# First output projection and norm inside the last attention group, weight splits later

## The chip, the cores and the metric

One core of one Trainium2 chip runs the whole program. The metric is the device time of a launch in microseconds (us), the median of several runs.

## The reference

A post-norm decoder layer on 2 sequences of 1024 tokens, width 256, in float32:

```python
x = _layernorm(x + attn(x, WQ, WK, WV, WO))          # causal, 16 heads of 16
x = _layernorm(x + xattn(x, ctx, ctx, mask, Wq, ...))  # 64 context keys per sequence
x = _layernorm(x + ffn(x, gate_w, gate_b, w13, w2, w13_s, w2_s))
```

The feed-forward part routes each token to 4 of 16 experts (sigmoid scores plus a bias, top 4, weights normalised and scaled by 2.5) and adds a shared expert. An expert is `(silu(x W1) * (x W3)) W2` with an inner width of 128.

## The kernel before

Each engine has its own program, in an order written out by hand, and they meet by semaphores. Tokens lie in 16 tiles of 128, eight for each sequence. The stages are these.

Causal attention runs over NG = 8 groups of four heads, four groups for each sequence. In a group, `step_order` lists 24 "B" steps (score blocks, line 1509), after which ScalarE takes the exponential (792), GpSimd cuts the diagonal blocks (680), and every second step TensorE multiplies by the values ("V", `product`, 1533). Between them stand the row maxima of the next group ("A": TensorE 1492 and 1497, VectorE 957), so the last group has none. Each group's row sums go to DRAM and back (`sums` on SyncE, 493 to 512), with VectorE's reciprocal between ("R" at step 14, line 947), and `normalise` on GpSimd (686, 689) scales the group two groups later, and adds each odd group to the even one before it, raising `o_done`. The last group is scaled and added by VectorE (1051, 1055).

Behind the last group stand the key and value projections of cross-attention (1584, 1588) and the tile loop over all 16 tiles. Per tile t: TensorE's output projection (1608, banks 0 and 1), which needs `o_done` of its sequence; VectorE's residual addition and statistics (`norm_stats`, 1025 to 1031); GpSimd's `power` (714); VectorE's `norm_apply` (1036); TensorE's transpose into a bank (`transpose_x`, 1598, three tiles later); ScalarE's copy into x_T (824); and after every fourth tile a query projection (1624) that ScalarE keeps with its bias (831). VectorE also turns keys and values into block form there, in 20 pieces (`keep_kv`, 1010 and 1018), over tiles 5 to 14.

The expert weights are loaded after the last group (SyncE, 553 to 564). Each of 17 experts (the last is the shared one) is split in two parts: `w_high` on ScalarE (817, two instructions) and then `w_low` on GpSimd (721, two instructions). With W_TILE = 4 and W_LAG = 4, ScalarE splits experts 0 to 11 at tiles 4 to 15, GpSimd 0 to 7 at tiles 8 to 15; the others follow in cross-attention.

Cross-attention runs in the order of `x_order`: 32 steps (two for each tile), each kind of work lagging behind the scores "S" by its number of steps in `LAGS`. ScalarE has an exponential (864) and a copy (871) at each step; GpSimd adds the output bias (740) at the first 16 steps, has a `w_low` at odd steps, and `power` of the second norm at "Y"; VectorE's `norm_shift` (1074) needs this power, ScalarE's apply (881) needs that, and TensorE's transpose "X" (1598) needs the apply. Routing, the scatter of tokens (755), the experts' blocks and the last norm follow.

On each engine an instruction that waits holds up all behind it.

## Time and profile before

| | us |
|---|---|
| median of 3 runs | 721.92 |
| lowest, highest | 718.9, 725.09 |
| the profiled run, its time | 721.0 |
| its span in the trace | 719.2 |
| busy in the span: TensorE | 608.2 (85%) |
| VectorE | 480.7 (67%) |
| ScalarE | 361.3 (50%) |
| GpSimd | 323.4 (45%) |

The share of busy time is an average over stages. For the change, what counts is the stretch from the start of the last group, at about 280.6 us, to the middle of cross-attention, at about 400 us. The largest entries of the chain of waits by line are TensorE's matmuls of lines 1533, 1509 and 1492, those of attention.

### The profile page before, as it was taken

Reading aid. Unit: us, or ns where it says so; the run is one execution under the profiler, and the core shown is the slowest. Engines: PE = TensorE matmul, PEld = TensorE weight load, DVE = VectorE, ACT = ScalarE, POOL = GpSimd, SP = SyncE. Lnnn points to the kernel's source line nnn. Section 1 sums busy time; section 2 is a strip of 40 time slices with the busy share of each in tenths; the row PEclk is TensorE's granted clock in tenths of the full one; section 3 lists DMA queues with packets and bytes.
Section 4 is the critical chain, followed back from the end, with each engine's and each line's share of the span. In section 5 each row is a group of like instructions: output and inputs, shape, how many; then the busy total and the mean of one; then the engine's idle time right before and its main releaser. Section 6 shows DMA issues by size and latency. Waiting matters only on the chain.

```text
span 719.2 us, 12945 instructions
## 1 busy us (share of the span) xinstructions
PE 608.2 (85%) x3852; PEld 370.8 (52%) x3852; DVE 480.7 (67%) x1310; ACT 361.3 (50%) x745; POOL 323.4 (45%) x397
## 2 busy tenths in 40 slices
PE   5888899999999998988799897965345888888874
PEld 2534443444434432255377675755344777777741
DVE  0378878889788783089478856555425776778676
ACT  1322376666665767725465443423313565556552
POOL 8414212335233433629656373746164455555430
PEclk9999999999999999999999996969676999999998
DMA  5866866527246100068000020212154765467756
GB/s 164 175 170 137 161 209 90 81 43 92 53 56 97 27 4 19 17 209 305 1 1 1 0 96 32 88 40 92 55 171 126 204 197 169 138 179 239 239 186 224
DMA packets 52114, 82.51 MB, mean 115 GB/s; under 512 B 11937, under 2 KB 29601, under 8 KB 51745
## 3 DMA queue, kind: packets, MB, share of 16 engines
q1 hardware_dynamic: 45184, 62.26, 35.4%
q0 software_dynamic: 6864, 19.44, 7.4%
q8 instruction: 34, 0.56, 0.3%
q14 instruction: 32, 0.25, 0.1%
HBM read 53.38 MB, written 32.48 MB: 119 GB/s over the span
## 4 chain that ended last, share of the span: by engine, by line
PE 55%; DVE 17%; issue 8%; another core or an unknown queue 6%; ACT 5%; DMA 4%; POOL 3%; SPq 1%; DVEq 0%; ACTq 0%; POOLq 0%
PE ps L1533 9%; PE ps L1509 8%; PE ps L1492 7%; PE ps L1803 6%; DVE neg_max L957 6%; PE ps L1826 5%; PE ps L1699 3%; PE ps L1718 3%; PE ps L1497 2%; PE ps L1782 2%; PE ps L1708 1%; POOL stacks L647 1%; PE ps L1735 1%; DMA expert_parts<-expert_outputs 1%
## 5 line engine op out<-in xcount | busy, mean ns | idle before, releaser
L957 DVE TENSOR_REDUCE neg_max<-ps 128x1 f32<-128x512 f32 (+3 forms) x304 | 181.5, 654 | 41.4 <-PE ps L1497 25.2
L792 ACT ACTIVATE temps<-ps 128x1024 f32<-128x1024 f32 (+1 forms) x192 | 147.5, 812 | 78.0 <-PE ps L1509 78.0
L680 POOL TENSOR_SCALAR_AFFINE_SELECT temps<-temps 128x256 f32<-128x256 f32 x128 | 52.1, 410 | 148.2 <-ACT temps L792 147.2
L1492 PE MATMUL ps<-stacks 96*128 96x512 bf16 (+3 forms) x384 | 104.5, 328 | 10.3 <-DVE neg_max L957 4.7
L762 POOL DMA_INDIRECT expert_outputs<-x_T,w_o_xqkv x79 | 76.1, 963 | 75.6 <-ACT x_T L930 45.0
L1509 PE MATMUL ps<-stacks 99*128 99x512 bf16 (+3 forms) x384 | 93.3, 328 | 2.9 <-DMA stacks<-m_rows 1.4
L1533 PE MATMUL ps<-temps,v_group 128*32 128x512 f32 (+3 forms) x768 | 81.8, 497 | 1.6 <-POOL temps L680 1.0
L755 POOL DMA_INDIRECT expert_slots<-x_tok,w_o_xqkv x64 | 62.4, 974 | 35.4 <-DVE w_o_xqkv L1142 17.9
L1803 PE MATMUL ps<-w_split,block_x 128*128 x474 | 71.3, 287 | 0.8 <-DVE block_x L1379 0.8
L1509 PEld LDWEIGHTS ps<-stacks 99*128 99x128 bf16 x384 | 26.9, 97 | 75.0 <-ACT temps L792 49.6
L1826 PE MATMUL ps<-w_split,block_h 128*128 x237 | 50.7, 323 | 17.5 <-DVE block_h L1406 11.5
L1803 PEld LDWEIGHTS ps<-w_split,block_x 128*128 128x128 f32 x474 | 63.1, 192 | 1.5 <-issue 1.3
L1492 PEld LDWEIGHTS ps<-stacks 96*128 96x128 bf16 x384 | 36.8, 97 | 47.9 <-DVE neg_max L957 21.2
L1402 DVE TENSOR_TENSOR o_norm<-ps,o_norm 128x128 f32<-128x128 f32 x79 | 22.9, 290 | 46.9 <-ACT o_norm L917 35.8
L917 ACT ACTIVATE o_norm<-ps 128x128 f32<-128x128 f32 x79 | 21.9, 278 | 56.1 <-PE ps L1803 33.0
L1826 PEld LDWEIGHTS ps<-w_split,block_h 128*128 128x128 f32 x237 | 34.8, 193 | 29.5 <-issue 26.8
L1497 PE MATMUL ps<-caus_a,ident_b 128*128 128x128 bf16 x256 | 49.8, 221 | 0.0
L714 POOL TENSOR_TENSOR ln_rstd<-ln_var_eps,minus_half 128x1 f32<-128x1 f32 x32 | 19.8, 618 | 65.1 <-DVE ln_var_eps L1031 65.1
L864 ACT ACTIVATE o_norm<-o_norm 128x512 f32<-128x512 f32 x32 | 20.2, 630 | 46.2 <-DVE o_norm L1291 43.5
L930 ACT ACTIVATE x_T<-ps,w_o_xqkv 128x256 f32<-128x256 f32 x60 | 28.6, 477 | 20.3 <-PE ps L1826 16.9
L1547 PE MATMUL ps<-x_T,w_qkv 128*128 128x512 f32 x64 | 32.5, 649 | 7.5 <-DMA x_T<-in_xT 7.5
L1379 DVE TENSOR_TENSOR block_x<-ps,block_x 128x256 fp32r<-128x256 f32 x79 | 33.4, 423 | 7.6 <-issue 3.3
(221 smaller groups left out, 1105.9 us busy)
## 6 DMA issues: line engine op xcount, KB each, us to landing
stacks<-qk_parts SPq DMA_DIRECT2D x96, 128.0 KB, 5.9
v_group<-expert_slots SPq DMA_DIRECT2D x79, 138.5 KB
qk_parts<-temps SPq DMA_DIRECT2D x8, 768.0 KB, 4.4
w_raw<-in_w SPq DMA_DIRECT2D x4, 1024.0 KB, 10.7
early_parts<-expert_outputs SPq DMA_DIRECT2D x4, 1024.0 KB
expert_slots<-in_pad SPq DMA_DIRECT2D x16, 138.5 KB
expert_slots<-in_pad SPq DMA_DIRECT2D x1, 2077.5 KB
x_T<-in_xT SPq DMA_DIRECT2D x4, 512.0 KB, 7.6
```

The costliest lines, as they stand in the source:

```text
L680: nc.gpsimd.affine_select(diag, diag, [[0, 2], [1, P]], ALU.is_ge, zero, base=0, channel_multiplier=-1).then_inc(b_cut, 1)
L755: pool.indirect_dma_start(slots, bass.IndirectOffsetOnAxis(ridx[:, t, k:k + 1].bitcast(U32), 0), xe[:, t, :], None).then_inc(scattered[q], 16)
L762: pool.indirect_dma_start(sums_of, bass.IndirectOffsetOnAxis(idxs[:, b:b + 1].bitcast(U32), 0), yb[:, b % YB, :], None).then_inc(landed[b ...
L792: nc.scalar.activation(pt[:, n % 4, :, 0:w], ps[:, 2 + 2 * (n % 2):4 + 2 * (n % 2), 0:w], ACT.Exp, scale=SCALE).then_inc(b_exp, 1)
L957: nc.vector.tensor_reduce(nmx[:, c, h0:h0 + nh, i], ps[:, A_BANKS[n % 3], 0:w * nh].rearrange("p (h k) -> p h k", h=nh), axis=AX.X, op=ALU ...
L1379: nc.vector.tensor_tensor(xsp[b % 3][:, 1].rearrange("p k s -> p (k s)"), ps[:, b % 2, 0:D], xsp[b % 3][:, 0].rearrange("p k s -> p (k s)" ...
L1492: last = nc.tensor.matmul(ps[:, A_BANKS[n % 3], w * s:w * s + w], qs[0:KR, ua, h0 + s, P * i:P * i + P], ks[0:KR, ua, h0 + s, CH * c:CH * ...
L1497: last = nc.tensor.matmul(ps[:, A_BANKS[n % 3], w * (s + 1) - P:w * (s + 1)], identb[:], causA[:], start=False, stop=True)
L1509: last = nc.tensor.matmul(ps[:, bank, 0:w], ks[0:KM, u, 2 * pr + s, P * j:P * j + P], qs[0:KM, u, 2 * pr + s, q0:q0 + w], start=True, stop ...
L1533: last = nc.tensor.matmul(ps[HS * h:HS * h + HS, 6, CH - w:CH], vg[:, u, j, h, :], pt[:, (2 * p + h // 2) % 4, h % 2, 0:w], start=(j == 0) ...
L1803: last = nc.tensor.matmul(ps[:, 2 + b % 2, 0:D], xsp[b % 3][:, xp, k, :], w13s[:, bass.ds(expert[b], 1), wp, at:at + 2 * INTER], start=(k ...
L1826: last = nc.tensor.matmul(ps[:, 6 + b % 2, 0:D], hsp[:, b % 3, hp, :], w2s[:, bass.ds(expert[b], 1), wp, :], start=(n == 0), stop=(n == 2))
```

## The change

Tiles 0 to 7 (the first sequence, whose groups are complete) are taken into the last group: at odd steps n, tile (n-1)/2 gets "LY" (projection and statistics), tile (n-3)/2 "LZ" (apply), tile (n-5)/2 "LX" (transpose into bank 7, copied to x_T by VectorE, not by ScalarE). GpSimd's `power` stands behind the diagonal cuts of the same steps, and the scaling of group 5 at step 8. The reciprocal "R" of group 6 keeps step 14. The tile loop runs over tiles 8 to 15 alone. Before it, TensorE makes the first two query projections and VectorE all 20 `keep_kv` pieces, the reciprocal and the two passes over the last group. W_TILE becomes 12 and W_LAG 1: ScalarE splits experts 0 to 3 in the tile loop and 4 to 16 in cross-attention, GpSimd 0 to 2 and 3 to 16, two experts at each odd step up to 13.

Functions that are only moved are left out of the diff (`power`, `norm_stats`, `norm_apply`, `transpose_x` are unchanged).

```diff
--- before.py
+++ after.py
@@ -123,6 +123,8 @@
             out.append(("V", (n - 3) // 2))
         if n == 2 * C0 + 1:
             out.append(("O", 0))
+        if g == NG - 1 and n % 2:
+            out += [(kind, (n - at) // 2) for kind, at in (("LY", 1), ("LZ", 3), ("LX", 5)) if 0 <= n - at < 2 * TB]
     return out
 
 
@@ -441,7 +443,6 @@
 
             return (1, b // 4 + 1) if b % 4 == 3 else (0, b + 1 - (b + 1) // 4)
 
-        KV_TILES = (5, 15)
         LN3_BASE = 2 * NT
         ADDS = ((0, 4), (4, 2), (6, 2), (8, 4), (12, 2), (14, 2))
         FINAL8 = NB1 + E
@@ -454,7 +455,7 @@
             t, n = ADDS[c]
             return lineb[c - 1][:] if c in (1, 2) else accb[:, :, t:t + n, :]
         STATS_END = [3 * LN3_BASE + sum(2 * n + 1 for _, n in ADDS[:c + 1]) for c in range(len(ADDS))]
-        W_TILE, W_LAG = 4, 4
+        W_TILE, W_LAG = 12, 1
         W_ACT, W_POOL = NT - W_TILE, NT - W_TILE - W_LAG
         SHARED = E
 
@@ -688,7 +689,12 @@
                     pool.wait_ge(o_scaled, g + 1)
                     nc.gpsimd.tensor_tensor(on[:, g, :], on[:, g, :], on[:, g - 1, :], ALU.add).then_inc(o_done, 1)
 
-            for g in range(NG):
+            def power(n):
+                pool.wait_ge(ln_chain, 3 * n + 3)
+                nc.gpsimd.tensor_tensor(rstd[:, n % 4:n % 4 + 1], ve[:, n % 4:n % 4 + 1], half[:],
+                                        ALU.pow).then_inc(ln_pow, 1)
+
+            for g in range(NG - 1):
                 for n in DIAG[:2 * C0]:
                     cut(g, n)
                 if 1 <= g < NG - 2:
@@ -701,6 +707,13 @@
                     normalise(g - 2)
                 for n in DIAG[2 * C0:]:
                     cut(g, n)
+            for n in range(NB):
+                if n in DIAG:
+                    cut(NG - 1, n)
+                if n == 2 * C0:
+                    normalise(NG - 3)
+                if n % 2 and 0 <= n - 3 < 2 * TB:
+                    power((n - 3) // 2)
             normalise(NG - 2)
             pool.wait_ge(vg_ready, NG)
             pool.wait_ge(pv_done, NV * NG)
@@ -709,11 +722,6 @@
                 pool.wait_ge(filled, 9 + d)
                 nc.gpsimd.memset(vbd[S2 * d:S2 * d + S2, :, :, VW * d + DH:VW * d + VW], 1.0).then_inc(filled, 1)
 
...
             def w_low(e):
 
                 pool.wait_ge(w_hi, 2 * e + 2)
@@ -727,7 +735,7 @@
                 nc.gpsimd.tensor_tensor(xs_l[:, :, CH * c:CH * c + CH], xT[:, :, CH * c:CH * c + CH],
                                         xs_h[:, :, CH * c:CH * c + CH], ALU.subtract).then_inc(xs_lo, 1)
 
-            for t in range(NT):
+            for t in range(TB, NT):
                 power(t)
                 if t >= W_TILE + W_LAG:
                     w_low(t - W_TILE - W_LAG)
@@ -738,8 +746,9 @@
                 if kind == "S" and n < NT:
                     pool.wait_ge(xT_kept, n + 1)
                     nc.gpsimd.tensor_tensor(x[:, n, :], x[:, n, :], bo, ALU.add).then_inc(bo_added, 1)
-                if kind == "S" and n % 2 and W_POOL + n // 2 <= E:
-                    w_low(W_POOL + n // 2)
+                if kind == "S" and n % 2:
+                    for e in range(W_POOL + n - 1, min(W_POOL + n + 1, E + 1)):
+                        w_low(e)
                 if kind == "Y":
                     power(NT + n)
                 if kind == "M":
@@ -816,7 +825,16 @@
                 for raw, high in zip(raw_of(e), part_of(e, 0)):
                     nc.scalar.activation(high, raw, ACT.Copy).then_inc(w_hi, 1)
 
-            for t in range(NT + 1):
+            def keep_query(c):
+
+                for o in range(2):
+                    act.wait_ge(xq_ready, 2 * c + o + 1)
+                    nc.scalar.activation(q2[:, o, CH * c:CH * c + CH], ps[:, 6 + o, :],
+                                         ACT.Identity, bias=bq[:, o:o + 1]).then_inc(xq_kept, 1)
+
+            keep_query(0)
+            keep_query(1)
+            for t in range(TB, NT + 1):
                 if W_TILE <= t < NT:
                     w_high(t - W_TILE)
                 if t < NT:
@@ -824,12 +842,9 @@
                     nc.scalar.activation(xT[:, :, P * t:P * t + P],
                                          ps[:, 2 + t % 2, 0:D].rearrange("p (c s) -> p c s", c=KC),
                                          ACT.Copy).then_inc(xT_kept, 1)
-                if t and t % 4 == 0:
-                    for o in range(2):
-                        n = (t // 4 - 1) * 2 + o
-                        act.wait_ge(xq_ready, n + 1)
-                        nc.scalar.activation(q2[:, o, CH * (t // 4 - 1):CH * (t // 4)], ps[:, 6 + o, :],
-                                             ACT.Identity, bias=bq[:, o:o + 1]).then_inc(xq_kept, 1)
+                if t > TB and t % 4 == 0:
+                    keep_query(t // 4 - 1)
+
             def shared(c):
                 act.wait_ge(g_ready, c + 1)
                 wait(act, h_done, c - 1)
@@ -862,8 +877,9 @@
                     if n >= 2:
                         act.wait_ge(xpT_ready, n - 1)
                     nc.scalar.activation(px[:, n % 2, :], sx[:, n % 2, :], ACT.Exp, scale=SCALE).then_inc(xp_exp, 1)
-                    if n % 2 and W_ACT + n // 2 <= E:
-                        w_high(W_ACT + n // 2)
+                    if n % 2:
+                        for e in range(W_ACT + n - 1, min(W_ACT + n + 1, E + 1)):
+                            w_high(e)
                 if kind == "T":
                     act.wait_ge(xpT_ready, n + 1)
                     if n >= 2:
@@ -942,6 +958,25 @@
         @block.vector
         def _(dve):
             dve.wait_ge(filled, 7)
+
...
             def recip(g, slot):
                 dve.wait_ge(l_moved, 48 * g + 32)
                 nc.vector.reciprocal(lrec[:, slot, :], lsum[:, slot, :]).then_inc(l_recip, 1)
@@ -959,6 +994,17 @@
                                                 axis=AX.X, op=ALU.max, negate=True).then_inc(a_max, 1)
                     if kind == "R":
                         recip(g - 1, (g - 1) % 3)
+                    if kind == "LY":
+                        if n == 0:
+                            dve.wait_ge(ld_late, 16 * 16)
+                        dve.wait_ge(y_ready, n + 1)
+                        norm_stats(n, ps[:, n % 2, 0:D], n, n % 4)
+                    if kind == "LZ":
+                        norm_apply(n, n, n % 4)
+                    if kind == "LX":
+                        dve.wait_ge(xT_ready, n + 1)
+                        nc.vector.tensor_copy(xT[:, :, P * n:P * n + P],
+                                              ps[:, 7, 0:D].rearrange("p (c s) -> p c s", c=KC)).then_inc(xT_kept, 1)
                     if kind == "M":
 
                         base = (g + 1) * 4
@@ -1018,46 +1064,21 @@
                     nc.vector.tensor_tensor(vbd[rows, b, :, VW * d:VW * d + DH], src, bias,
                                             ALU.add).then_inc(kv_kept, 1)
 
...
-            for t in range(NT + 1):
-                if KV_TILES[0] <= t < KV_TILES[1]:
-                    span = KV_TILES[1] - KV_TILES[0]
-                    at = t - KV_TILES[0]
-                    for piece in range(20 * at // span, 20 * (at + 1) // span):
-                        keep_kv(piece)
-                if t == 1:
-                    dve.wait_ge(l_moved, 48 * (NG - 1) + 32)
-                    nc.vector.reciprocal(lrec[:, (NG - 1) % 3, :], lsum[:, (NG - 1) % 3, :]).then_inc(l_recip, 1)
-                if t == 6:
-
-                    dve.wait_ge(l_spread[(NG - 1) % 2], 64 * (NG // 2))
-                    nc.vector.tensor_tensor(on[:, NG - 1, :], on[:, NG - 1, :], rl[:, (NG - 1) % 2, :],
-                                            ALU.mult).then_inc(o_scaled, 1)
-                if t == 7:
-                    dve.wait_ge(o_scaled, NG)
-                    nc.vector.tensor_tensor(on[:, NG - 1, :], on[:, NG - 1, :], on[:, NG - 2, :],
-                                            ALU.add).then_inc(o_done, 1)
+            for piece in range(4):
+                keep_kv(piece)
+            recip(NG - 1, (NG - 1) % 3)
+            for piece in range(4, 20):
+                keep_kv(piece)
+            dve.wait_ge(l_spread[(NG - 1) % 2], 64 * (NG // 2))
+            nc.vector.tensor_tensor(on[:, NG - 1, :], on[:, NG - 1, :], rl[:, (NG - 1) % 2, :],
+                                    ALU.mult).then_inc(o_scaled, 1)
+            dve.wait_ge(o_scaled, NG)
+            nc.vector.tensor_tensor(on[:, NG - 1, :], on[:, NG - 1, :], on[:, NG - 2, :], ALU.add).then_inc(o_done, 1)
+            for t in range(TB, NT + 1):
                 if t < NT:
                     dve.wait_ge(y_ready, t + 1)
                     norm_stats(t, ps[:, t % 2, 0:D], t, t % 4)
-                if t >= 1:
+                if t > TB:
                     norm_apply(t - 1, t - 1, (t - 1) % 4)
 
             steps = [0]
@@ -1474,6 +1495,32 @@
 
         @block.tensor
         def _(pe):
+            def transpose_x(t, bank):
+                for k in range(KC):
+                    last = nc.tensor.transpose(ps[:, bank, P * k:P * k + P], x[:, t, P * k:P * k + P], identf[:])
+                last.then_inc(xT_ready, 1)
+
+            def out_project(t):
+
+                pe.wait_ge(o_done, (t // TB + 1) * GB // 2)
+                if t >= 2:
+                    pe.wait_ge(ln_in, t - 1)
+                for q in range(GB // 2):
+                    pair = on[:, t // TB * GB + 2 * q + 1, P * (t % TB):P * (t % TB) + P]
+                    last = nc.tensor.matmul(ps[:, t % 2, 0:D], pair, wo1[:, q, :], start=(q == 0),
+                                            stop=(q == GB // 2 - 1))
+                last.then_inc(y_ready, 1)
+
+            def query_project(c):
+
+                for o in range(2):
+                    if c:
+                        pe.wait_ge(xq_kept, 2 * c + o - 1)
+                    for k in range(KC):
+                        last = nc.tensor.matmul(ps[:, 6 + o, :], wxq[:, k, P * o:P * o + P],
+                                                xT[:, k, CH * c:CH * c + CH], start=(k == 0), stop=(k == KC - 1))
+                    last.then_inc(xq_ready, 1)
+
             def group(g, order):
 
                 u = g % 3
@@ -1509,6 +1556,16 @@
                             last = nc.tensor.matmul(ps[:, bank, 0:w], ks[0:KM, u, 2 * pr + s, P * j:P * j + P],
                                                     qs[0:KM, u, 2 * pr + s, q0:q0 + w], start=True, stop=True)
                         last.then_inc(b_ready, 1)
+                    if kind == "LY":
+                        if n == 0:
+                            pe.wait_ge(ld_late, 16 * 16)
+                            pe.wait_ge(a_max, NA * NG)
+                            pe.wait_ge(m_row, NG)
+                        out_project(n)
+                    if kind == "LX":
+                        pe.wait_ge(ln_done, n + 1)
+                        wait(pe, xT_kept, n)
+                        transpose_x(n, 7)
                     if kind in ("V", "Vp"):
                         product(g * NV + (0 if kind == "V" else -NV), g if kind == "V" else g - 1,
                                 u if kind == "V" else (g - 1) % 3, n)
@@ -1593,37 +1650,21 @@
             pe.wait_ge(o_kept, 2 * NG)
             pe.wait_ge(m_row, NG)
 
...
+            pe.wait_ge(xT_kept, TB)
+            query_project(0)
+            query_project(1)
+            for t in range(TB, NT + 4):
                 if t < NT:
-                    if t >= 2:
-                        pe.wait_ge(ln_in, t - 1)
-                    pe.wait_ge(o_done, (t // TB + 1) * GB // 2)
-                    for q in range(GB // 2):
-                        pair = on[:, t // TB * GB + 2 * q + 1, P * (t % TB):P * (t % TB) + P]
-                        last = nc.tensor.matmul(ps[:, t % 2, 0:D], pair, wo1[:, q, :], start=(q == 0),
-                                                stop=(q == GB // 2 - 1))
-                    last.then_inc(y_ready, 1)
+                    out_project(t)
                 s = t - 3
-                if 0 <= s < NT:
+                if TB <= s < NT:
                     pe.wait_ge(ln_done, s + 1)
-                    if s >= 2:
-                        pe.wait_ge(xT_kept, s - 1)
+                    pe.wait_ge(xT_kept, max(s - 1, TB))
                     transpose_x(s, 2 + s % 2)
                 s -= 1
-                if s >= 0 and s % 4 == 3:
+                if s >= TB and s % 4 == 3:
                     pe.wait_ge(xT_kept, s + 1)
-                    for o in range(2):
-                        if s >= 4:
-                            pe.wait_ge(xq_kept, s // 4 * 2 + o - 1)
-                        for k in range(KC):
-                            last = nc.tensor.matmul(ps[:, 6 + o, :], wxq[:, k, P * o:P * o + P],
-                                                    xT[:, k, P * (s - 3):P * (s + 1)], start=(k == 0), stop=(k == KC - 1))
-                        last.then_inc(xq_ready, 1)
+                    query_project(s // 4)
 
             def project(c, part):
 
```

## Rows read from the trace of the kernel before

**Rows 1.** Busy time by engine, stretch by stretch: a full group, then the last group.
```profile
222.90:251.75 28.85, 28.02 (x220) 11.73 (x217) 23.34 (x44) 19.21 (x27) 11.49 (x18) 1.00 0.49 67
...
280.60:303.80 23.20, 20.35 (x153) 5.37 (x153) 1.07 (x2) 18.86 (x26) 12.06 (x19) 1.00 0.05 14
```

**Rows 2.** Timeline, TensorE in the tile loop: start us, us, engine, line, operation.
```profile
323.56 0.38 PE L1598 MATMUL ps<-ident_f,x_tok 128*128 128x128 f32 x2
...
323.78 1.03 PE L1608 MATMUL ps<-w_o_xqkv,o_norm 128*128 128x256 f32 x4
...
324.64 0.38 PE L1598 MATMUL ps<-ident_f,x_tok 128*128 128x128 f32 x2
```

**Rows 3.** Timeline inside the last group: GpSimd's normalisation of group 5, ScalarE's exponentials.
```profile
288.45 2.35 POOL L686 TENSOR_TENSOR o_norm<-o_norm,temps 128x1024 f32<-128x1024 f32 x1
...
290.57 3.85 ACT L792 ACTIVATE temps<-ps 128x1024 f32<-128x1024 f32 x4
```

**Rows 4.** Row sums of the last group: timeline, and the landing time of L511.
```profile
303.91 0.60 ACT L807 ACTIVATE o_norm<-ps 128x512 f32<-128x512 f32 x1 [1.19 <-PE ps L1533]
...
310.68 1.71 SPq L511 DMA_DIRECT2D temps<-row_sums  x4
...
DMA to landing us min/median/max: 2.1/2.5/3.5
```

**Rows 5.** Timeline of the tile loop: key/value products, VectorE's tile, keep_kv, scaling, one query block.
```profile
304.77 1.89 PE L1588 MATMUL ps<-w_o_xqkv,ctx_T 128*128 128x256 f32 x8
...
310.60 0.42 DVE L1025 TENSOR_TENSOR x_tok<-ps,x_tok 128x256 f32<-128x256 f32 x1
...
312.12 0.42 DVE L1025 TENSOR_TENSOR x_tok<-ps,x_tok 128x256 f32<-128x256 f32 x1
...
315.17 0.72 DVE L1010 TENSOR_SCALAR v_group<-ps,b_k,head_mask 128x128 f32<-128x128 f32 x2
...
317.96 1.22 DVE L1051 TENSOR_TENSOR o_norm<-o_norm,temps 128x1024 f32<-128x1024 f32 x1
...
338.91 3.60 PE L1624 MATMUL ps<-x_T,w_o_xqkv 128*128 128x512 f32 x8
```

**Rows 6.** Timeline of the end of the tile loop, and its two stretches by engine.
```profile
342.55 0.69 ACT L831 ACTIVATE o_norm<-ps,b_q 128x512 f32<-128x512 f32 x1 [1.03 <-PE ps L1624]
...
343.13 0.92 ACT L817 ACTIVATE w_split<-w_raw 128x512 fp32r<-128x512 f32 x2
...
343.91 2.00 POOL L721 TENSOR_TENSOR w_split<-w_raw,w_split 128x512 fp32r<-128x512 f32 x2
...
343.98 1.35 DVE L1036 TENSOR_SCALAR x_tok<-x_tok,ln_mean_var,ln_rstd 128x256 f32<-128x256 f32 x1 [1.13 <-POOL ln_rstd L714]
...
346.57 5.28 PE L1624 MATMUL ps<-x_T,w_o_xqkv 128*128 128x512 f32 x8 [0.75 <-ACT x_T L824]
...
352.83 1.10 PE L1699 MATMUL ps<-v_group,o_norm 128*128 128x512 f32 x2 [0.97 <-ACT o_norm L831]
...
346.50:352.00 5.50, 5.28 (x8) 2.08 (x8) 0.00 (x0) 0.81 (x3) 0.08 (x1) 0.70 0.00 0
```

**Rows 7.** Timeline of the start of cross-attention, up to its second tile's transpose.
```profile
352.24 1.41 POOL L740 TENSOR_TENSOR x_tok<-x_tok,w_qkv 128x256 f32<-128x256 f32 x2
...
357.49 0.92 ACT L817 ACTIVATE w_split<-w_raw 128x512 fp32r<-128x512 f32 x2
...
371.02 0.55 POOL L714 TENSOR_TENSOR ln_rstd<-ln_var_eps,minus_half 128x1 f32<-128x1 f32 x1 [5.94 <-DVE ln_var_eps L1031]
...
372.30 0.63 ACT L864 ACTIVATE o_norm<-o_norm 128x512 f32<-128x512 f32 x1 [1.46 <-DVE o_norm L1291]
...
373.57 0.60 ACT L881 ACTIVATE x_tok<-x_tok,ln_minus_mean,ln_rstd 128x256 f32<-128x256 f32 x1
...
375.30 0.38 PE L1598 MATMUL ps<-ident_f,x_tok 128*128 128x128 f32 x2
...
381.37 0.38 PE L1598 MATMUL ps<-ident_f,x_tok 128*128 128x128 f32 x2
```

39 lines of the change are left out of this document (15 added, 24 removed).

## The prediction

> **What bounds the kernel now.** I read the forty slices of the page first, for where TensorE is full; then the chain of waits, for which lines carry the time around the change; then stretches by engine; then the timeline of the same stretches. [rows 1] shows, behind each stretch's length, the busy time of TensorE's matmuls, its weight loads, VectorE, ScalarE and GpSimd, then the granted clock: a full attention group has TensorE busy for 28.02 of 28.85 us. The last group builds no maxima for a next one: 20.35 of 23.20 us, VectorE 1.07, ScalarE 18.86 [rows 1]. So it has 2.85 us of idle TensorE and an almost empty VectorE, the room that the change fills. The group ends at 303.8 [rows 1], cross-attention's first score is at 352.83 [rows 6]: 49.0 us of tile loop, in which VectorE's chain per tile sets the pace, 1.52 us from one addition to the next (310.60 to 312.12) [rows 5]. In cross-attention TensorE is the bound: 6.07 us a tile, from transpose to transpose (375.30 to 381.37) [rows 7].
>
> **Step 1, the last group grows.** TensorE gets eight output projections and eight transposes. Behind one another they take 323.56 to 323.78 for the transpose and 323.78 to 324.64 for the projection, so 1.08 us a tile [rows 2], 8.6 us for eight. Walked through in its new order, the first projection falls into a wait for ScalarE and costs nothing (0.9 back). From step 4 to 19 TensorE is behind instead, since two full exponentials take 1.9 us (3.85 for four) [rows 3] and what TensorE does meanwhile is over 3 us; there all is paid. Two of the x_T copies, which VectorE makes in order behind the next tile's statistics, come 0.3 us late (0.6 more), and of the other 1.95 us idle about half, 0.9, is filled while TensorE is behind: 8.6 - 0.9 + 0.6 - 0.9 = **+7.4 us**. Bounds: all idle time filled, 8.6 - 2.85 = +5.8, and 1 less if products also overlap better; +10 if normalise stalls it. GpSimd does that at step 8: 2.35 us [rows 3] and an addition over as many elements, 4.7 us together, ahead of power(3). I place power(3)'s result within 0.5 us of where the transpose of tile 3 is due, so the stall is small, but behind it in TensorE's queue stand the next scores, and for these ScalarE waits. ScalarE itself loses nothing: it has no added instruction there.
>
> The row of one apply shows another meeting: it took 1.35 us beside GpSimd's subtraction of 343.91 [rows 6]. [...]
>
> **Step 2, what the first eight tiles covered.** Group 7's row sums go over DRAM and back: ScalarE's copy at 303.91, the spread issued from 310.68 for 1.71 us, landing 2.5 us after its last issue (about 312.0): 314.5 [rows 4]. That is 10.7 us after the group's end, and about 10.0 when the reciprocal no longer stands behind tiles' statistics. Before, the tiles hid it all. Now TensorE has the key/value products (to 304.77 + 1.89 = 306.7, 2.8 us after the end, its last 0.1 overlapping what follows) and two query blocks, 3.5 us each (3.60 for a block with its tail) [rows 5]: busy to +9.7. VectorE has twenty keep_kv pieces of about 0.36 us (0.72 for two) [rows 5], done by +10.2: these are hidden by the chain. Then the two passes over the whole group, 1.22 us each [rows 5], and o_done at +12.7. TensorE stands still for 3 us.
>
> **Step 3, tiles 8 to 15.** First addition at +13.9, the others every 1.52 us [rows 5]: tile 15's at +24.2, its statistics by +25.3 if nothing stood in the way. But the wait moves to the splits. The loop's ScalarE order is w_high(0), copy 12, keep_query(2), w_high(1). The third query block cannot start before the copy of tile 11, +23.2, and ends at +26.7; keep_query takes 0.69, w_high(1) 0.92 [rows 6]: +28.4. With W_LAG at 1, GpSimd has w_low(1) in front of power(15), where before it was four experts behind and never waited. 2.00 us [rows 6] later power(15), 0.6: +31.0. The apply takes 0.4 to 1.35 [rows 6] beside w_low(2), the transpose and copy 1.2, the last query block 5.28 at the low clock [rows 6], and one more us to the first score (351.85 to 352.83): **+39.0 us** where it was 49.0, so **-10.0**. Bounds: with the last block at the full clock and the apply undisturbed +36.5 (-12.5), and one us better still if VectorE's tiles run below 1.52; +40.5 (-8.5) if the clock is low from the 3 us standstill on.
>
> [...]
>
> **Step 4, cross-attention takes the splits.** ScalarE's splits there go from 5 experts to 13, GpSimd's from 9 to 14, two at every odd step up to 13. GpSimd per tile: two additions of bo 1.41, two splits 4.0 (2.00 each [rows 6]), power 0.55 [rows 7]: 5.8 to 6.0 us against 6.07 [rows 7]. It only just fits, and the start does not: in front of power(16) stand eight bo additions and eight splits. 352.24 to 353.6 the first two additions, w_low(3) to 355.6, then w_low(4) waits for w_high(4), which ends at about 358.5 since ScalarE starts splits at 357.49 [rows 7]; w_low(4) is done at 360.5, three more rounds of two additions and two splits, 5.3 us each, end at 376.4, and power(16) is done at 376.9 instead of 371.57 [rows 7]. ScalarE's apply needs it; it ran at 373.57 and could have run at 374.3 without TensorE's transpose at 375.30 [rows 7] moving, given that a projection is in front of it. With about 1.0 us by which ScalarE's double splits delay the first steps, the transpose comes at 377.7 to 378.3. Behind that wait in TensorE's queue is the next tile's score; behind VectorE's wait for power(16) are the maxima of step 9. One later round adds 0.4. **+3.0 us** (bounds: +1, if ScalarE's and GpSimd's idle time takes it, to +6, the whole 5.3 of GpSimd's lateness and a little).
>
> In the later stretches nothing is added, and since TensorE is full there a shift goes through to the end. Of the eight experts' splits that leave the tile loop nothing is counted on ScalarE, where copies waited for transposes; GpSimd's part of their gain is in step 3.
>
> **The sum.** +7.4 - 10.0 + 3.0 = +0.4 us on the profiled span of 719.2 us, whose run took 721.0; on the median 721.92, 722.3. I say **722 us**. About 1%, 7.2 us, is what a measurement of this kernel can tell from no change.
>
> **Rivals.**
> (a) No measurable change, as above: 0.60. For it: three terms of like size and opposite sign. It holds where the terms stay within their bounds, 716.5 to 727.
> (b) Faster, 713: the idle time of the last group is all filled (+5.3), the loop ends at full clock with the splits out of the way (-13.5), cross-attention pays 1. Sum -7.2 to -9. For it: VectorE is 95% idle in the last group [rows 1]. Against: keep_query(2) stands before w_high(1). 0.17.
> (c) Slower, 729: ScalarE. The second split stands between the exponential of an odd step and the copy that TensorE's next product needs. ScalarE waited 1.46 us before the exponential of step 8 [rows 7]; the second split takes 0.92 of it [rows 6]. If at a step less than 0.92 is left, TensorE stops there, and once a tile: 7 x 0.92 = 6.4 more, 722.3 + 6.4 = 728.7. It decides where ScalarE's idle time per tile falls under 0.92; the 1.46 speaks against. 0.23, with other losses of the same sign.
> The range reaches from (b) to (c): 714 to 729. Likeliest alone: 716.5 to 727. Faster by over 1% 0.17, within 1% 0.60, slower by over 1% 0.23.
>
> **What would show it.** Step 1: the last group's length, 30 to 31 us; its ScalarE idle before exponentials with TensorE as releaser. Under 28.5 or over 33 it is wrong. Step 2: an idle stretch of TensorE of about 3 us after the second query block, ended by VectorE's addition (line 1055 before). Step 3: power(15) starting as w_low(1) ends, and 39 us from group's end to first score. Step 4: power of the first cross tile starting at once behind a split, some 24 us after GpSimd's first bo addition, VectorE waiting for it, and a period of 6.1 us after. What breaks the forecast: a group that swallows the tiles in under 5 us, or cross-attention whose period goes to 7.

## The result and the profile after

| | kernel before, us | changed kernel, us | ratio, 95% interval |
|---|---|---|---|
| median of 7 runs each | 722.9 | 729.61 | 1.0097 [1.0068, 1.0126] |
| lowest, highest | 718.9, 725.09 | 725.9, 733.33 | |
| span of the profiled execution | 719.2 | 727.5 | |

The change costs 6.7 us where 0 was forecast: just outside the range. The same two kernels on another chip gave 1.0118 [1.0032, 1.0203].

The spans by stage, read from the timelines. "First score" is the first of cross-attention; X0, X1 and "last X" are TensorE's transposes of its first, second and last tile, counted from the first score.

| kernel | last group | group's end to first score | X0 | X1 | last X |
|---|---|---|---|---|---|
| before | 23.2 | 49.1 | +22.5 | +28.5 | +141.5 |
| changed | 30.7 | 40.2 | +27.3 | +35.6 | +148.9 |
| difference | +7.5 | -8.9 | +4.8 | +7.1 | +7.4 |

7.5 - 8.9 + 7.4 = 6.0 of the profiled spans' 8.3; most of the rest (2.5) arises in the expert stage, whose length from its first product with split weights to the end was 196.6 and 191.6 us in two profiles of the changed kernel. A second profile of the kernel before, on another chip (before_again), has 23.2, 50.4, +22.5, +28.5 and +139.7: the stretch to the first score and the last X vary by 1 to 2 us in one and the same kernel, the other columns hardly. First the group and what follows, by engine (length, then busy time of TensorE, its weight loads, VectorE, ScalarE, GpSimd, and the granted clock), as in [rows 1]:

```profile
280.30:311.00 30.70, 29.35 (x201) 13.40 (x201) 16.85 (x50) 19.02 (x26) 16.32 (x27) 1.00 0.05 11
343.00:351.10 8.10, 6.69 (x10) 2.63 (x10) 0.00 (x0) 1.76 (x3) 1.39 (x3) 0.64 0.08 33
```

The group holds 9.0 us more TensorE work than in [rows 1], and 1.5 us of its idle time went into that. The timeline of the loop's end, answering to [rows 5, 6]:

```profile
322.17 1.23 DVE L1076 TENSOR_TENSOR o_norm<-o_norm 128x1024 f32<-128x1024 f32 x1
323.45 4.06 PE L1510 MATMUL ps<-w_o_xqkv,o_norm 128*128 128x256 f32 x16 [2.75 <-DVE o_norm L1076]
324.62 0.42 DVE L966 TENSOR_TENSOR x_tok<-ps,x_tok 128x256 f32<-128x256 f32 x1 [1.22 <-PE ps L1510]
...
339.09 1.96 POOL L729 TENSOR_TENSOR w_split<-w_raw,w_split 128x512 fp32r<-128x512 f32 x2 [2.67 <-ACT w_split L826]
341.00 0.56 POOL L694 TENSOR_TENSOR ln_rstd<-ln_var_eps,minus_half 128x1 f32<-128x1 f32 x1
...
341.59 1.35 DVE L977 TENSOR_SCALAR x_tok<-x_tok,ln_mean_var,ln_rstd 128x256 f32<-128x256 f32 x1 [4.72 <-POOL ln_rstd L694]
...
344.15 6.00 PE L1520 MATMUL ps<-x_T,w_o_xqkv 128*128 128x512 f32 x8 [0.47 <-ACT x_T L842]
```

GpSimd's w_low(1) waits 2.67 us for ScalarE, power(15) stands right behind it, and VectorE's last apply waits 4.72 us for that power. The last query projection then takes 6.00 us, at a stretch's clock of 0.64. The start of cross-attention, answering to [rows 7], and the same three instructions at its second tile:

```profile
356.80 1.95 POOL L729 TENSOR_TENSOR w_split<-w_raw,w_split 128x512 fp32r<-128x512 f32 x2 [2.93 <-ACT w_split L826]
...
370.12 3.88 POOL L729 TENSOR_TENSOR w_split<-w_raw,w_split 128x512 fp32r<-128x512 f32 x4
373.94 0.56 POOL L694 TENSOR_TENSOR ln_rstd<-ln_var_eps,minus_half 128x1 f32<-128x1 f32 x1
374.46 1.41 POOL L748 TENSOR_TENSOR x_tok<-x_tok,w_qkv 128x256 f32<-128x256 f32 x2
375.81 1.96 POOL L729 TENSOR_TENSOR w_split<-w_raw,w_split 128x512 fp32r<-128x512 f32 x2
...
374.54 3.25 DVE L1095 SCALAR_TENSOR_TENSOR ln_minus_mean<-ln_mean_var,ln_rstd 128x1 f32<-128x1 f32 x1 [3.18 <-POOL ln_rstd L694]
...
377.82 0.60 ACT L897 ACTIVATE x_tok<-x_tok,ln_minus_mean,ln_rstd 128x256 f32<-128x256 f32 x1 [5.04 <-DVE ln_minus_mean L1095]
...
378.48 0.69 PE L1500 MATMUL ps<-ident_f,x_tok 128*128 128x128 f32 x2 [3.92 <-ACT x_tok L897]
378.96 1.92 PE L1740 MATMUL ps<-v_group,o_norm 128*128 128x512 f32 x2
...
382.60 0.55 POOL L694 TENSOR_TENSOR ln_rstd<-ln_var_eps,minus_half 128x1 f32<-128x1 f32 x1
383.12 1.23 POOL L748 TENSOR_TENSOR x_tok<-x_tok,w_qkv 128x256 f32<-128x256 f32 x2
...
383.18 0.59 DVE L1095 SCALAR_TENSOR_TENSOR ln_minus_mean<-ln_mean_var,ln_rstd 128x1 f32<-128x1 f32 x1 [0.43 <-POOL ln_rstd L694]
```

Read it downwards: the power of the first tile is done 22.8 + 0.6 us behind the first score instead of 18.2 + 0.6. VectorE then makes one column of numbers, 128x1 (`norm_shift`, "the shift" below), and it takes 3.25 us, while GpSimd's two additions (374.46) and the two halves of a split (375.81) run beside it, one behind the other; it ends at 377.79, as GpSimd runs out of work at 377.77. In the kernel before it took 0.15:

```profile
372.18 0.15 DVE L1074 SCALAR_TENSOR_TENSOR ln_minus_mean<-ln_mean_var,ln_rstd 128x1 f32<-128x1 f32 x1
```

The first tile is an exception, though. At the second tile GpSimd's two additions also stand one behind the other, and the shift ends with the first of them, after 0.59 us. At the first tile ScalarE's apply waits for the shift, TensorE stands still ahead of the transpose for 3.92 us, and what follows runs slower, at a granted clock of 0.51 from 376.1 to 383.0: the scores of line 1740 take 1.92 us where they took 1.10 before [rows 6]. X1 comes 8.3 us behind X0, not 6.07 [rows 7]. The third and the fourth tile come 6.1 us apart again, as before the change.

### The profile page after: what moved, and what is told of

Same layout as the page of the kernel before. It is cut to its first block, busy times and chain, and to the rows that moved or that the text cites. A ratio compares the mean times of both kernels' runs of the same rounds, so it can differ in the third digit from the quotient of the medians.

```text
span 727.5 us, 12948 instructions
## 1 busy us (share of the span) xinstructions
PE 609.2 (84%) x3852; PEld 373.9 (51%) x3852; DVE 486.0 (67%) x1318; ACT 359.4 (49%) x737; POOL 323.0 (44%) x397
## 4 chain that ended last, share of the span: by engine, by line
PE 56%; DVE 15%; issue 7%; POOL 6%; another core or an unknown queue 6%; DMA 5%; ACT 4%; SPq 1%; DVEq 0%; ACTq 0%; POOLq 0%
PE ps L1590 9%; PE ps L1556 8%; PE ps L1539 7%; PE ps L1844 6%; DVE neg_max L992 5%; PE ps L1867 5%; PE ps L1740 2%; PE ps L1759 2%; PE ps L1510 2%; POOL w_split L729 2%; PE ps L1823 2%; PE ps L1544 2%; POOL stacks L648 1%; PE ps L1520 1%
## 5 line engine op out<-in xcount | busy, mean ns | idle before, releaser
L1423 DVE TENSOR_TENSOR o_norm<-ps,o_norm 128x128 f32<-128x128 f32 x79 | 22.8, 289 | 47.9 <-issue 23.5
```

## The experiments

The runs went to several chips. On one kind (kind A here: this result, the first four experiments, and before_again, after_again, warm4 and before_shift) the kernel before takes 718 to 723 us, on the other (kind B: all others) 673. Every ratio is to the kernel before on the same chip. Both kinds agree up to the eighth tile of cross-attention; the difference behind it is told in the last section. The changed kernel itself was timed on kind A alone, tiles_only and shadow on kind B alone.

**The splits of cross-attention.** Three edits, and the weights' part alone.

```diff
 single_both: one expert at an odd step on both engines
-                    for e in range(W_POOL + n - 1, min(W_POOL + n + 1, E + 1)):
+                    for e in range(W_POOL + n // 2, min(W_POOL + n // 2 + 1, E + 1)):
                         w_low(e)
 (and the same for w_high); act_double: that for w_low alone
 ...
 shift_first: the changed kernel, with
                     power(NT + n)
+                    pool.wait_ge(ln_shift, n + 1)
 ...
 weights_only: the kernel before, with W_TILE, W_LAG = 12, 1 and two experts at odd steps
```

> The changed kernel, but in cross-attention each engine splits one expert at an odd step (ScalarE up to step 25, GpSimd up to step 27) instead of two. The group and the tile loop stay. Theory (the loss sits in GpSimd's doubled splits in front of the first power of cross-attention, and in what VectorE's norm_shift then waits for): from the first cross score to the transpose of cross tile 1 it takes about 28.5 us as before the change, not 35.6, and the time falls to 722 to 725 us, less if five splits among the scatters cost nothing, more by up to 10 if all do. Rival (the loss is in the group and the tile loop or is spread): 728 to 730, the stretch 33 us or more.

> The changed kernel with ScalarE's splits doubled as they are, GpSimd's one at an odd step. Theory (GpSimd): like single_both within 1 us, stretch from first score to second transpose about 29 to 30 us, 723 to 726 us. Rival (ScalarE's second split between exponential and copy holds TensorE): that stretch stays above 33 us and the time at 728 to 730.

> The changed kernel, and GpSimd waits behind each cross power until VectorE's norm_shift of that tile is done, so that no GpSimd work on SBUF runs beside it. Theory: norm_shift took 3.25 us at cross tile 0 because additions and a split held it up; it falls to about 0.2 us, the first cross transpose comes about 3 us sooner, 726 to 727 us. Rival (norm_shift's 3.25 us is only how a wait is recorded, or GpSimd's own delay gives it back): no change, 729 to 730.

> The kernel before with the later splits alone (W_TILE 12, W_LAG 1, two experts at an odd step); all 16 tiles stay in the tile loop. Theory: the tile loop loses GpSimd's splits from eight tiles and shortens by 4 to 7 us (from group's end to first score 42 to 45 us, not 49), cross-attention pays about 7: 722 to 726 us. Rival (the splits cost nothing in cross-attention by themselves, only together with the tiles): 715 to 718.

| kernel | group | to first score | X0 | X1 | last X | ratio |
|---|---|---|---|---|---|---|
| single_both | 30.7 | 41.0 | +22.5 | +28.5 | +145.2 | 1.004 [1.0012, 1.0068] |
| act_double | 30.7 | 42.7 | +23.3 | +29.3 | +142.8 | 1.0026 [0.9988, 1.0063] |
| shift_first | 30.7 | 40.8 | +24.3 | +30.5 | +145.9 | 1.0014 [0.998, 1.0048] |
| weights_only | 23.2 | 50.8 | +27.4 | +35.7 | +148.9 | 1.0144 [1.0096, 1.0192] |

The steps between these kernels take 6.9 of the 7.1 us of X1 apart. Single splits on both: nothing lost (22.5, 28.5). ScalarE's doubles: 0.8 (23.3). GpSimd's doubles, with VectorE's shift kept clear of them: 1.0 more (24.3). The shift beside GpSimd's work: 3.0 more (27.3). The step from X0 to X1: 6.2 in shift_first, 8.3 in the changed kernel, 2.1 more. In shift_first the same instruction takes 0.16 us, with GpSimd's additions held until it is done:

```profile
375.97 0.16 DVE L1096 SCALAR_TENSOR_TENSOR ln_minus_mean<-ln_mean_var,ln_rstd 128x1 f32<-128x1 f32 x1 [3.18 <-POOL ln_rstd L694]
...
376.21 1.40 POOL L748 TENSOR_TENSOR x_tok<-x_tok,w_qkv 128x256 f32<-128x256 f32 x2 [0.27 <-DVE ln_minus_mean L1096]
```

So GpSimd's work beside the shift is the cause of its 3.25 us. Why it lasted over four instructions is open: all six profiles in which the first power stands behind the doubled subtractions and GpSimd does not wait for the shift show 3.25 or 3.26 us at the first tile, and nowhere else. In the 99 other cases in all these profiles in which an arithmetic operation of GpSimd was running as a shift began, the shift ended within 0.1 us of the end of that operation, whatever stood behind it.

Two limits of this table. The first three kernels run the changed kernel's code up to the first score, and still need 40.8 to 42.7 us where it needed 40.2: behind the standstill ahead of tile 8 the first sixteen products took 4.06 us in the changed kernel and in shift_first, 5.41 in the other two:

```profile
327.47 5.41 PE L1510 MATMUL ps<-w_o_xqkv,o_norm 128*128 128x256 f32 x16 [3.53 <-DVE o_norm L1076]
```

This line is act_double's; the granted clock was 0.53 from 327.5 to 330.0, and 1.00 over the 4.06 us of the changed kernel. And behind the second tile all three lose again, last X +142.8 to +145.9 for +141.5 and +139.7 in the kernel before, which these runs don't take apart.

weights_only missed my expectation on its loop, which I had thought would get shorter. It has the changed kernel's wait in the tile loop too: ScalarE reaches w_high(1) late, and VectorE's last apply stands behind it.

```profile
344.42 1.34 DVE L1038 TENSOR_SCALAR x_tok<-x_tok,ln_mean_var,ln_rstd 128x256 f32<-128x256 f32 x1 [4.05 <-POOL ln_rstd L714]
```

So the weights' part alone costs 1.4%, more than the whole change, and the tiles' part gives back about 0.5% of it, though the two intervals overlap.

**TensorE's clock behind the standstill.** warm and warm4 put 14 and 4 products of 512 columns, results not used, ahead of TensorE's wait for X0 (the edit of warm4; in warm 14 stands for 4):

```diff
                 if kind == "X":
+                    for _ in range(4 if n == 0 else 0):
+                        nc.tensor.matmul(ps[:, 7, :], q2[:, 0, 0:P], kbd[:, 0, 0].rearrange("p h k -> p (h k)"),
+                                         start=True, stop=True)
                     pe.wait_ge(ln_done, NT + n + 1)
```

> The changed kernel with 14 more matmuls of 512 columns on TensorE (results not used) ahead of its wait for the first cross-attention tile's normalised rows, in the standstill of 3.92 us there. Theory (of the delay of the first cross tiles 2.1 us is TensorE's clock, which is at the lower level behind the standstill, so that the second tile comes 8.3 us behind the first instead of 6.1): with TensorE busy until shortly before the transpose, the first transpose stays at 27 to 28 us behind the first score, the second follows after 6.1 to 6.8 us instead of 8.3, and the later tiles stand about 2 us sooner; the time falls by 0 to 2 us, to 727.5 to 729.6. Rival (the 8.3 us come from the queues behind VectorE and ScalarE, whatever the clock): the distance stays 8 us or more.

> The changed kernel with 4 instead of 14 more products of 512 columns (results not used) on TensorE ahead of its wait for the first cross-attention tile: the 14 ran 12.18 us and so held the engine themselves, 4 take 3.5 us, less than the standstill of 3.92 us. Theory (2.1 us of the first tiles' delay is TensorE's clock behind the standstill): the first transpose stays at 27 to 28 us behind the first score, the second follows after 6.1 to 6.8 us and not 8.3, and the time is 0 to 2 us below that of the changed kernel. Rival (the 8.3 us come from the work queued on VectorE and ScalarE, whatever the clock): the distance stays 8 us or more.

warm says nothing on the clock: I had mis-sized the filler, which took 12.18 us and itself put X0 at +35.3 (ratio 1.0172 [1.0123, 1.0221]). warm4 (kind A) settles it:

```profile
377.29 3.60 PE L1781 MATMUL ps<-v_group,o_norm 128*128 128x512 f32 x8
381.37 0.44 PE L1500 MATMUL ps<-ident_f,x_tok 128*128 128x128 f32 x2 [0.48 <-ACT x_tok L897]
381.64 1.02 PE L1740 MATMUL ps<-v_group,o_norm 128*128 128x512 f32 x2
```

X0 at +27.4 as before the filler, X1 at +33.6: 6.2 us and not 8.3, and line 1740 back at 1.02 us; the granted clock was 1.00 from 377.0 to 387.6. Work that computes nothing gave 2.1 us back. (Its profile reached the first score after 42.1 us, with 6.38 us for the sixteen products named above, so the gain is read from X0 to X1 and not from the sum.) Beside it on the same chip ran the changed kernel:

> The changed kernel, word for word, beside the others on the same chip. Theory (the change costs what it costs in the attention, whatever the expert stage takes): the last group 30.7 us, the loop 40.2, the first transposes 27.3 and 35.6 us behind the first score, and a ratio to the kernel before of about 1.010 (the 6.7 us of the first chip). Rival (the quicker chip hides or shows another part of it): a ratio of 1.005 or less, or of 1.015 or more.

It showed 30.7, 40.2, +27.3 and +35.7 and a ratio of 1.0118 [1.0032, 1.0203], warm4 1.007 [1.0027, 1.0113]: the right direction and size, but the two times can't be told apart.

**The wait in the tile loop.** late_power: all powers first, then the three subtractions.

```diff
             for t in range(TB, NT):
                 power(t)
-                if t >= W_TILE + W_LAG:
-                    w_low(t - W_TILE - W_LAG)
+            for e in range(NT - W_TILE - W_LAG):
+                w_low(e)
```

> One edit to the changed kernel: behind the tile loop's copies GpSimd computes all eight powers of the second batch's tiles first and only then the three subtractions of the weight splits, so power(15) no longer stands behind w_low(1), which waits for ScalarE's w_high(1). Theory (the loop gave 8.9 and not more because VectorE's last apply waited 4.72 us for that power): the wait of 4.72 us is gone, the last query projection starts some 4 to 5 us sooner, the stretch from the end of the last group to the first score falls from 40.2 to 35 to 37 us, and the time falls from 729.6 to about 725. Rival (ScalarE's 0.92 us splits and copies set the end of the loop anyway, or the projection then runs longer at the lower clock): the stretch stays above 39 us and the time at 728 to 730. Cross-attention starts with the same double splits, so its tiles should stay where they were, the first transpose of a tile 27 us behind the first score and the second 35 us behind it.

```profile
338.41 1.35 DVE L977 TENSOR_SCALAR x_tok<-x_tok,ln_mean_var,ln_rstd 128x256 f32<-128x256 f32 x1 [0.44 <-POOL ln_rstd L694]
...
341.66 0.94 ACT L826 ACTIVATE w_split<-w_raw 128x512 fp32r<-128x512 f32 x2
342.49 0.38 ACT L842 ACTIVATE x_T<-ps 128x256 f32<-128x256 f32 x1
...
342.92 5.29 PE L1520 MATMUL ps<-x_T,w_o_xqkv 128*128 128x512 f32 x8 [1.69 <-ACT x_T L842]
```

The 4.72 us are gone (0.44), yet the stretch is 38.2, 2.0 shorter and not 3 to 5: the last query projection starts 1.2 us sooner and takes 5.29 us for 6.00. The wait moved to ScalarE, whose last copy stands behind three splits of 0.9 us: the rival was half right. Ratio, kind B: 1.0062 [1.0015, 1.0108]; whether that is a gain isn't shown, since the changed kernel was not timed there.

**The tiles' part with the splits spread out.** W_TILE, W_LAG = 8, 4 and one expert at an odd step; run twice on kind B, the second time with a profile of the kernel before beside it.

> The tiles' part of the change with as little of the weights' part as the shorter loop leaves: ScalarE makes 8 high parts in the loop's tiles 8 to 15, GpSimd 4 low parts with a lag of 4 tiles, and cross-attention makes one of each at an odd step, as before the change. Theory (the tiles' part gains and the weights' part costs): the last group stays 30.7 us, the loop falls to 36 to 39 us (no power behind a subtraction that waits), the first transposes of cross-attention stand 22.5 and 28.5 us behind the first score as before, and the time is 716 to 720, below the kernel before. Rival (the eight tiles in the group cost as much as they save): the time is 722 or more even with the splits spread out.

> The tiles' part of the change with the splits spread out, for a second time. Theory (it gains about 4 us by the first score and loses them in cross-attention's later tiles, where VectorE and GpSimd carry routing, scatters and the splits that the shorter loop pushed behind it): the first score comes 3 to 5 us before that of the kernel before on this chip, the transposes of the first four tiles stand alike, and the last stands 3 to 6 us later behind the first score; the ratio is 1.000 to 1.006. Rival (the loss lies behind the last tile or in the expert stage): the last transpose stands within 1.5 us of that of the kernel before, and the stretches behind it are longer. Second rival (the loss on the other chip was the scatter of the runs): the ratio is 0.993 to 0.997.

| kernel | group | to first score | X0 | X1 | last X | ratio |
|---|---|---|---|---|---|---|
| before_third | 23.2 | 49.2 | +22.5 | +28.5 | +130.4 | |
| tiles_only | 30.7 | 37.6 | +22.5 | +28.5 | +137.9 | 1.0053 [1.0022, 1.0083] |
| tiles_again | 30.7 | 39.7 | +22.5 | +28.5 | +138.0 | 1.0056 [1.0019, 1.0093] |

2.0 to 4.1 us sooner at the first score, alike for four tiles, then 7.5 us lost. My forecast of a time below the kernel before fell: the splits that the shorter loop pushes on end at step 25 on GpSimd (step 17 before), where its queue holds routing's scatters and the powers. Ninth to tenth tile of tiles_again, 11.4 us for 7.5; the shift takes 2.30 us beside GpSimd's 128x1024 subtraction:

```profile
438.73 1.95 POOL L729 TENSOR_TENSOR s_split<-s_raw,s_split 128x512 fp32r<-128x512 f32 x2
440.64 0.57 POOL L694 TENSOR_TENSOR ln_rstd<-ln_var_eps,minus_half 128x1 f32<-128x1 f32 x1
441.19 2.33 POOL L735 TENSOR_TENSOR x_low<-x_T,x_high 128x1024 fp32r<-128x1024 f32 x1
...
441.24 2.30 DVE L1095 SCALAR_TENSOR_TENSOR ln_minus_mean<-ln_mean_var,ln_rstd 128x1 f32<-128x1 f32 x1 [2.12 <-POOL ln_rstd L694]
...
444.23 0.69 PE L1500 MATMUL ps<-ident_f,x_tok 128*128 128x128 f32 x2 [2.02 <-ACT x_tok L897]
```

Another 2.5 us (1.7 in tiles_only) stand between the fourth and the fifth tile, where TensorE was busy throughout and the granted clock fell all the same, to 0.50 from 398 to 402. By stretch, the kernel before (before_third) and then tiles_again:

```profile
394.10:410.40 16.30, 15.80 (x104) 11.94 (x103) 13.40 (x48) 7.01 (x16) 5.34 (x5) 1.00 0.01 2
```

```profile
391.50:407.80 16.30, 16.30 (x90) 12.48 (x88) 11.45 (x39) 8.74 (x20) 6.93 (x7) 0.79 0.00 1
```

Why is open. Over the same 16.3 us the granted clock was 0.90 in tiles_only and after_again and 0.79 in before_shift_again, below; the first profile of the changed kernel, the same program as after_again, lost nothing there (7.8 us from the fourth to the fifth tile, as in the kernel before). So these 1.7 to 2.5 us can't be put down to the tiles' part; the other 5 to 6 us come later.

**A layout of the splits.** shadow: powers first; four subtractions behind them, beside the last query projection; six high parts at ScalarE's tiles 11 to 16; in cross-attention two experts at steps 1, 3 and 5 (ScalarE at 5: one), then one at an odd step to 17 and 19.

```diff
+        W_TILES = {11: (0,), 12: (1,), 13: (2,), 14: (3,), 15: (4,), 16: (5,)}
 ...
+            for e in range(4):
+                w_low(e)
```

> The changed kernel with the splits laid where the engines stand: powers first in the loop, four low parts behind them beside the last query projection, six high parts in ScalarE's tiles 11 to 16, and in cross-attention two at steps 1, 3 and 5 and one at an odd step after these. Theory (the double splits cost where they stand ahead of the first tile's power and additions, at steps 7 and later, not at steps 1 to 5, in which no tile of cross-attention is normalised yet): the stretch from the group to the first score is 33 to 36 us, the first transposes stand at 22.5 to 23.5 and 28.5 to 29.5 us behind the first score as in the kernel before, and the time is 713 to 718. Rival (the doubles at steps 1 to 5 hold ScalarE's exponentials and so the first scores): the first transposes stand at 25 us or more and the time is 720 or more.

> The splits laid beside the last query projection and at cross-attention's steps 1, 3 and 5, for a second time. It reached the first score 35.2 us behind the last group and its last transpose stood 132.6 us behind the first score. Theory (its splits are out of the way before the routing begins): the last transpose stands 2 us or more sooner behind the first score than in the tiles' part alone, the ratio is again 0.990 to 0.998. Rival (the first result was the scatter of the runs): 1.000 or more.

> The changed tiles' order with the splits laid beside the last query projection and at cross-attention's steps 1, 3 and 5. On a chip on which the kernel before takes 718 to 722 us: the layout's gain by the first score (6 us of the two profiles: 5 to 8) stands, its later tiles come 1 to 3 us late, ratio 0.991 to 0.998; rival: the waits behind ScalarE's table loads, 28 to 30 us of cross-attention there, shift with the tiles and take the gain, ratio 0.999 or more. On a chip on which the kernel before takes 673 us: again 0.992 to 0.998.

It reached the first score 35.2, 38.7 and 37.2 us behind the group, X0 at +23.2 or +23.3, last X at +132.6, +131.6 and +132.6, with ratios of 0.9945 [0.9907, 0.9982], 0.996 [0.9924, 0.9996] and 0.9985 [0.9952, 1.0017] on three chips of kind B. It is the best form of the change, 0.15 to 0.55% faster than the kernel before on kind B, in the last run not told from it: at best the edge of what I expected (713 to 718 of 722). On kind A it was not run. Of the 3.5 us by which its loop varies 2.8 are the last query projection's: 3.70 us in the first run, at a granted clock of 1.00, and 6.53 in the second, at 0.56 on the mean.

**GpSimd's wait for VectorE's shift, by itself.** The line of shift_first in the kernel before (before_shift, before_shift_again) and in shadow (shadow_shift).

> The kernel before with one more wait on GpSimd: behind the power of a cross-attention tile it waits until VectorE's shift of that tile is made. In the changed kernel this wait gave 3 us at the first tile, where VectorE's shift took 3.25 us beside GpSimd's additions; in the kernel before the first shift took 0.15 us. Theory (only the changed kernel's doubled splits put GpSimd's work beside the first shift): the first tiles stay at 22.5 and 28.5 us, and the time within 1.5 us of the kernel before. Rival (the wait helps the later tiles as well, since there too shifts take over 3 us beside GpSimd's work): the later transposes come 2 us or more sooner and the time is 2 to 4 us lower.

> The kernel before with GpSimd's wait for VectorE's shift behind each power of a cross-attention tile. On a chip on which the kernel before takes 718 to 722 us: again 0.991 to 0.998, the stretch from the last transpose of a tile to the experts' first matmuls about 23.6 us instead of 28.6. On a chip on which it takes 673 us: there is no wait behind the table load to shorten, and in the laid-out kernel the same wait moved the last transpose from 131.6 to 137.9 us behind the first score, so a ratio of 1.004 to 1.012; rival (that loss belongs to the laid-out splits): 0.998 to 1.002.

> The same kernel with GpSimd's wait for VectorE's shift behind each power of a cross-attention tile. [...]

Kind A: 0.9945 [0.9906, 0.9985], faster than the kernel before with none of the change. Kind B: 1.01 [1.0063, 1.0137], and in shadow 1.0045 [0.9999, 1.0091]. On kind A the transposes did not move (last X +139.7 with it and +139.7 in before_again), and in the kernel before no shift took 3 us beside GpSimd's work. The gain lies behind the last transpose, in ScalarE's activation behind a table load. before_again, then before_shift:

```profile
495.14 1.28 ACT L891 ACT_TABLE_LOAD   x1
507.96 0.22 ACT L891 ACTIVATE w_o_xqkv<-ps 128x64 f32<-128x64 f32 x1 [11.54 <-remote]
```

```profile
494.41 1.28 ACT L892 ACT_TABLE_LOAD   x1
500.26 0.22 ACT L892 ACTIVATE w_o_xqkv<-ps 128x64 f32<-128x64 f32 x1 [4.57 <-remote]
```

So shift_first's good ratio (1.0014) is only in part the shift's 3 us won back; part is this: its longest wait at that activation is 5.3 us, the changed kernel's 13.2, and its experts' first product follows the last transpose after 25.9 us for 30.9. On kind B that wait is absent (2.76 us in before_third, ended by TensorE), and the transposes come later with the line (last X +134.9 for before_third's +130.4, and +137.9 in shadow_shift for shadow_again's +131.6). That the later start of the scatters does this is argued, not shown.

## Why the prediction was wrong

**Step 1** held: +7.4 forecast, +7.5 measured. That it is so near is partly luck: the added work was 9.0 us and not 8.6, and 1.5 us of idle time took it up where I had counted 1.2. Tile 2's apply took 1.29 us beside the 128x1024 multiplication of group 5 and tile 1's 0.49, so it lost 0.8; the multiplication, 2.35 us long, had begun 1.2 us earlier, and the apply ended 0.15 us behind it.

**Step 2** held: a standstill of TensorE of 3 us was forecast and 2.75 measured, the first addition forecast at +13.9 and measured at 324.62 - 310.9 = +13.7. What followed was kind to the forecast: behind the same standstill, of 2.6 to 3.7 us, the first sixteen products took 4.06 us in seven of the fourteen profiles with the tiles in the group, this one among them, and 5.41 or 6.38 in the other seven.

**Step 3** was near, -10.0 forecast, -8.9 measured. The wait was the one named, power(15) directly behind w_low(1), its result due at +31.0 and measured at 341.56 - 310.9 = +30.7. The rest is the last apply, 1.35 us beside w_low(2) where my sum leaves 0.5, and the last query projection, 6.00 us for 5.28. Two figures of the step don't follow from its own numbers: seven additions at 1.52 us behind +13.9 put tile 15's at +24.5, not +24.2, and the lower bound of +36.5 comes to +37.2; neither carries the forecast. No run shows the term behind the upper bound of +40.5, tiles slowed by a low clock from the standstill on: in this run the granted clock was 1.00 from 323.4 to 327.6, and in act_double, where it was 0.53 behind the standstill, the sixteen products took 5.41 us for 4.06. What I did not see: with the wait away, ScalarE's splits hold the loop almost as long (late_power).

**Step 4** is the step that failed: +3.0 forecast (+6 at most), +7.4 measured. Its GpSimd part was worked out well: power(16) forecast 5.3 us late, measured 4.6, and X0 would have come at +24.3 by that alone (shift_first), 1.8 us late where I had 2.4 to 3.0. The mis-sized term is what follows the power: I let ScalarE's apply need "it", and passed over VectorE's shift between the two, 0.15 us in the kernel before. Behind the late power it stands beside GpSimd's next additions and takes 3.25 us (3.0 lost at X0), and the standstill that it makes costs 2.1 more in clock. Both causes were in my text, for other places: the apply of 1.35 us beside a subtraction, and the last query block of 5.28 us, in a stretch with a granted clock of 0.70 [rows 6]. The first I had counted in step 3 and not in step 4. The shifts of the next three tiles took 0.59, 0.68 and 0.59 us, each ending with the GpSimd operation that was running as it began. An estimate on that pattern, from the first addition's end at 375.2, gives this shift about 0.7 us, so the pattern alone would not have given the 3.0 us: the shift ended after four GpSimd instructions, when GpSimd had nothing more to start.

**Rival (c)** gave 729 and the time was 729.61, but not by its mechanism: ScalarE's second split was to hold TensorE once a tile, and the tiles run at 6.1 us; ScalarE's doubles cost 0.8 us in all (act_double). Rival (b) had the group too cheap (+5.3 for +7.5), the loop too short (-13.5 for -8.9) and cross-attention at 1 us for 7.4.

**The account of where the gain went.** In the changed kernel the loop saves 8.9 us for the group's 7.5, a gain of only 1.4 us; with the splits spread out it is 2.0 to 4.1. Moving the splits pays for the shorter loop with work on GpSimd in cross-attention, in front of the powers at the start (changed kernel) or among the scatters later (tiles_only), and the last transpose comes some 7 us late either way. In front of the powers the runs show the cause. Among the scatters 1.7 to 2.5 us of it are a fall of the clock of unknown cause, and the rest is read from the queues: shadow, which differs from tiles_only in the splits alone, comes 1.2 to 2.2 us late instead of 7.5.

## What to carry to other kernels

Work moved off a critical stretch has to be placed against the queue that receives it: ask what stands behind it there, and put it where nothing that others wait for comes next. When a value becomes late, follow it through every small instruction to its user and look at what runs beside each at its new time; a 128x1 operation of 0.15 us became 3.25. And count a standstill of TensorE at its length and, as a risk, at a slower clock behind it: here 3.92 us, and 2.1 more at a granted clock of 0.51.

## What the runs showed of the hardware

- VectorE's 128x1 scalar_tensor_tensor took 0.15 or 0.16 us alone, 0.41 to 0.69 where it ended with the GpSimd operation that was running, 2.30 where that was a 128x1024 subtraction that had just begun, and 3.25 over four GpSimd instructions one behind the other, this at the first tile alone, in six profiles.
- A standstill of 3.92 us on TensorE was followed by work at a granted clock of 0.51 (changed kernel, 376.1 to 383.0), 2.1 us lost over one tile; 3.60 us of idle products in it gave them back. At one and the same place ahead of tile 8, a standstill of 2.75 us was followed by 4.06 us for sixteen products (changed kernel), one of 2.60 by 5.41 (shadow_again) and one of 2.89 by 4.06 (shift_first): the length alone does not decide. The granted clock also fell to 0.79 over 16.3 us without any idle time ahead of it (tiles_again).
- Two kinds of chips: 718 to 723 us and 673 us for the kernel before. In two profiles of the kernel before on kind A ScalarE spends 28.2 and 29.9 us of cross-attention in waits that no engine ends, in its profile on kind B none. The longest (11.54 and 13.10 us) stands at the activation shown above. No packet of an instruction queue lies in either of the two waits shown, and the next one comes only behind its end (from 508 to 509 in before_again, from 501 to 502 in before_shift). GpSimd's indirect stores run all through it, and the wait was 7 us shorter where that series of them started later (at 493.1 in before_shift, at 491.1 in before_again); what ends it is open, and no experiment moved the stores alone. The expert stage differs as well, 196 against 166 us, of unknown cause.
